# Attention 2's masks: two wide products or eight, replaced by four 64x64 tiles

## The chip, the core and the metric

The kernel runs on one core of a Trainium2 chip. The metric is device time in microseconds (us) of one execution of the whole program, four attention layers and four feed-forward layers, as the median of several runs.

PE is TensorE (PEld its weight loads), DVE VectorE, ACT ScalarE, POOL GpSimd, SP the queue that issues the transfers. SBUF is the working memory, PSUM the one that PE writes (eight banks of 512 f32 columns on 128 partitions).

## The reference

Eight blocks are added to `x` (16 sequences, 128 positions, 128 columns) in turn, each on a layer norm of `x`. The change is in the third attention:

```python
def _L2_xattn_ref(query, key, value, mask, w_q, b_q, w_k, b_k, w_v, b_v, w_o, b_o):
    N_HEAD = 16
    ...
    Q = _split_heads(query @ w_q.T + b_q)
    K = _split_heads(key @ w_k.T + b_k)
    V = _split_heads(value @ w_v.T + b_v)
    scores = jnp.einsum('bhqd,bhkd->bhqk', Q, K) * scale
    scores = jnp.where(mask, -jnp.inf, scores)
    probs = jax.nn.softmax(scores, axis=-1)
    attn = jnp.einsum('bhqk,bhkd->bhqd', probs, V)
    ...
    return merged @ w_o.T + b_o
```

Query and key have 128 positions each, so that the mask of one sequence is 128x128, the same for all 16 heads. A head is 8 wide.

## The kernel before

The program is written by hand as one instruction stream per engine, with semaphores between them. There is no scheduler: the order on an engine is the order of the calls in its block, and an instruction that waits holds back all behind it on that engine. `wait` hangs a wait onto the engine's next instruction; `held` (L266 to L271) gives it a semaphore instruction of its own, which also counts up a semaphore `gate` that nobody reads.

Attention runs as a software pipeline over the 16 sequences, `pipeline(engine, attention_step(layer), ...)` (L222). Step t takes sequence t through its input side (`turn_xn`, `query`), sequence t-2 through the scores (M), t-3 through the turned scores (ST) and the products with the values (AV), and finishes t-4. Two steps of attention 2 are already run inside the feed-forward block before it. Steps 4 to 15 hold all five parts; the last ones have no new sequence.

For a step of attention 2, PE's order is

```python
if Do: AV(2, 1); AV(3, 1)
if Po: shift_turn()
if Mo: M(0)
if Po: ST(0)
if Do: out_turn()
if A: turn_xn()
if Mo: M(1)
if A: query()
if Do and layer == 2: att_turn()
if Po: ST(1)
if Do: out_project()
if Po: AV(0); AV(1)
```

M(0) and M(1) call `scores`, ST(0) and ST(1) `scores_t`; each fills two banks with eight heads, four in each.

- `scores` (L412) writes scores with queries on partitions into banks 0 and 1, of which DVE takes the maxima (L1559, two of 512 columns per call). The mask comes first: `neg_ident`, the identity times -2^100, is the weight and the mask, repeated four times, is streamed: one product of 128x512 for each bank (L417). Then eight products of 48 rows each add the scores (L423), alternately on the upper and the lower half of the array's rows.
- `scores_t` (L428) writes the same scores turned, with keys on partitions, into banks 2 and 3, shifted by the maxima, for ACT's exponential (L874). Here the mask is the weight and `neg_ident` is streamed: eight products of 128x128 (L434). Then products of 48 and 64 rows add the scores (L440) and the shift (L444).

`scores` waits for the maxima of the call before (`mx`); `scores_t` waits for the exponentials that read its banks before (`p`).

In between stand `shift_turn` (L526), `out_turn` (L558, waits for ACT's `att`, L937), `turn_xn` (L507), `query` (L512), `att_turn` (L564, waits for DVE's `att_t`, L1617), `out_project` (L589) and the AV products (L482, 9 columns of weights on each of four strips of the array, whose input `probs` ACT has just written).

DVE's order in a step is: the copy of the turned shift (L1595), the maxima of M(0), statistics of the next sequence (L1526 to L1530), `normalized` (L1613, L1617), the maxima of M(1), the shifts (L1587, L1589), the rest of the query (L1574), the output (L1541). Every fourth step (k % 4 == 0) begins with the statistics of its own sequence, which the output of the step before has to precede; POOL turns them into a deviation (L1197 to L1200), ACT normalizes with it (L931) and then copies `att` (L937).

POOL copies each sequence's mask from bytes (`mask_u8`, loaded once) to bf16 (`mask_bf`, four slots, L1219), then the values (`v_slot`, L1225), computes the next deviation, and splits the query (L1235, L1237). PE's M waits for the copy of its sequence, made two steps earlier (`v`).

The mask is loaded at the start on SP's queue, in the group `later`, as 16x128 pieces of 128 bytes for each of the 128 query positions; DVE waits for the whole group in step 2 of attention 0 (L1434).

Of the kernel before, what the change touches and what calls it, by code (L numbers as in the profile page):

```python
# [14 lines left out]
BF16 = mybir.dt.bfloat16  # L15
U8 = mybir.dt.uint8
# [5 lines left out]
B = 16  # L22
T = 128
D = 128
P = 128
SLOTS = 4
# [8 lines left out]
UNIT = 4  # L35
# [24 lines left out]
def build_kernel(nc, a, out, scratch_q, scratch_k):  # L60
    ctx = ExitStack()
    with ctx:
        def sb(name, shape, dt=F32):
            return ctx.enter_context(nc.sbuf_tensor(name, shape, dt))
# [4 lines left out]
        bank = [ctx.enter_context(nc.psum_tensor(f"bank{i}", [P, 512], F32)) for i in range(8)]  # L69
# [10 lines left out]
        def keep(name, src, shape, dt=F32, group=later):  # L80
            whole = consts[name] = sb("w_" + name, shape, dt)
            group.append((whole[:, :] if len(shape) == 2 else whole[:, :, :], src))
            return whole
# [17 lines left out]
        w2 = keep("w2", a["w2T"], [P, D])  # L101
        b31 = keep("b31", a["L3_ffn_b1"].partition_broadcast(P), [P, F1])
        s_ins = keep("s_ins", a["s_ins"].partition_broadcast(P), [P, 2])
        mask_u8 = keep("mask_u8", a["mask"].rearrange("b q k -> q b k"), [P, B, T], U8)
        BO0, BV1, BV2, BV3, BO2, BF2, B32 = range(7)
        x_sb = sb("x_sb", [P, B, D])
        x_in = a["x"].rearrange("b t d -> t b d")
# [4 lines left out]
        neg_ident = sb("neg_ident", [P, P], BF16)  # L112
# [32 lines left out]
        mx = sb("mx", [P, SLOTS, H1])  # L145
# [4 lines left out]
        rec = sb("rec", [P, SLOTS, H1])  # L150
        att = sb("att", [P, SLOTS, 512])
        att_t = sb("att_t", [P, SLOTS, 512])
        mask_bf = sb("mask_bf", [P, SLOTS, T], BF16)
        v_slot = sb("v_slot", [P, SLOTS, H1, D1 + 1])

        v3_slot = k_parts[:, :, :, :, :].rearrange("p s l j k -> p (s l j k)")[:, 0:SLOTS * 512].bitcast(F32)
# [59 lines left out]
        def wait(eng, s, value):  # L216

            if isinstance(value, int) and value <= 0:
                return
            eng.wait_ge(s, value)  # L220
# [47 lines left out]
        def held(eng, s, value):  # L268

            if isinstance(value, int) and value <= 0:  # L270
                return  # L271
            eng.wait_ge(s, value)
            eng.sem_inc(gate, 1)
# [99 lines left out]
        def _(pe):  # L373
            mm, tr = nc.tensor.matmul, nc.tensor.transpose
# [28 lines left out]
            def turn_probs(sm, n):  # L403

                for u in range(2):
# [3 lines left out]
                        last = tr(bank[2 + u][:, j * T:(j + 1) * T], probs_q[u][:, j * T:(j + 1) * T], ident[:, :])  # L409
                    last.then_inc(sm["st"], 1)  # L410

            def scores(sm, layer, n, s, v):  # L412

                wait(pe, sm["mx"], n)
                if layer == 2:
                    for r in range(2):
                        mm(bank[r][:, :], neg_ident[:, :],  # L417
                           mask_bf[:, s:s + 1, :].to_broadcast([P, UNIT, T]), start=True, stop=False,
                           skip_group_check=True)
                for j in range(UNIT):  # L420
                    for r in range(2):
                        rows, g = slice(64 * r, 64 * r + 6 * D1), v * UNIT + j
                        last = mm(bank[r][:, j * T:(j + 1) * T], q_stack[rows, s, g, :], k_stack[rows, s, g, :],  # L423
                                  start=layer == 1, stop=True, skip_group_check=True)
                        if j == UNIT - 1:
                            last.then_inc(sm["s"], 1)

            def scores_t(sm, layer, n, s, v):  # L428

                wait(pe, sm["p"], n)  # L430
                if layer == 2:
                    for r in range(2):
                        for j in range(UNIT):
                            mm(bank[2 + r][:, j * T:(j + 1) * T], mask_bf[:, s, :], neg_ident[:, :],  # L434
                               start=(j == 0), stop=False, skip_group_check=True)
                for j in range(UNIT):
                    g = v * UNIT + j
                    for r in range(2):
                        rows = slice(64 * r, 64 * r + 6 * D1)
                        mm(bank[2 + r][:, j * T:(j + 1) * T], k_stack[rows, s, g, :], q_stack[rows, s, g, :],  # L440
                           start=layer == 1, stop=False, skip_group_check=True)
                    for r in range(2):
                        rows = slice(64 * r, 64 * r + 64)
                        last = mm(bank[2 + r][:, j * T:(j + 1) * T], pick_bf[rows, g:g + 1].to_broadcast([64, T]),  # L444
                                  shift_t[rows, s, :], start=False, stop=True, skip_group_check=True)
                        if j == UNIT - 1:
                            last.then_inc(sm["st"], 1)
# [711 lines left out]
        def _(pool):  # L1159
# [26 lines left out]
            def attention_step(layer):  # L1186
                sm = S[layer]
                U = (H0 if layer in (0, 3) else H1) // UNIT
                def step(t, k, c):
                    s = k % SLOTS  # L1190
# [25 lines left out]
                    if layer:  # L1216
                        held(pool, sm["av"], (t - 3) * U)
                        if layer == 2:
                            nc.gpsimd.tensor_copy(mask_bf[:, s, :], mask_u8[:, t, :])  # L1219
                        if layer == 3:  # L1220
                            cp = nc.gpsimd.tensor_copy(
                                v3_slot[:, s, :, :, 0:D3].rearrange("p u j e -> p (u j) e"),
# [20 lines left out]
                    elif on(k, 1):  # L1243
                        s = (k - 1) % SLOTS
# [839 lines left out]
```

## Time and profile before

| | us |
|---|---|
| median of 3 runs | 861.32 |
| lowest, highest | 857.58, 863.76 |
| the profiled execution | 858.38 |
| its span, first to last instruction | 856.6 |

| engine | busy us | share of the span |
|---|---|---|
| PE | 581.3 | 68% |
| DVE | 536.8 | 63% |
| ACT | 399.4 | 47% |
| POOL | 255.4 | 30% |

Matmuls are pipelined: a 128-column product is shown with over 0.2 us though the next begins after 0.06, so that spacing, not duration, is what one costs. The clock column is the granted TensorE clock (1.00 is 2.4 GHz, 0.50 is 1.2 GHz). Idle time is put down to what ended last before the instruction began; "issue" is idle time with no such event. All times in rows count from the span's start.

### The profile page before, as it was taken

What the parts mean: (1) busy time and instruction counts of PE and PEld (TensorE: products, weight loads), DVE (VectorE), ACT (ScalarE), POOL (GpSimd) and SP (SyncE); (2) the same over time, 40 slices, a digit from 0 to 9 for tenths busy, and PEclk for the clock granted to TensorE, in tenths of its full rate; (3) what the DMA queues carried; (4) which work ended last, traced back from release to release, by engine and by line L of the source; (5) the groups of instructions that cost most, each with busy time, mean ns of one, the idle gap of its engine ahead of it and who ended that gap; (6) DMA issues with size and microseconds to landing.
All of it is one profiled execution on the core that took longest, in us unless ns stands there. A gap on an engine that the chain in (4) does not pass through costs nothing.

```text
span 856.6 us, 19147 instructions
## 1 busy us (share of the span) xinstructions
PE 581.3 (68%) x5772; PEld 400.5 (47%) x5772; DVE 536.8 (63%) x1653; ACT 399.4 (47%) x893; POOL 255.4 (30%) x515
## 2 busy tenths in 40 slices
PE   4599999987788857878513322699998027875342
PEld 3478787875444444545201101366665015653121
DVE  2477676752677746777688885366675663335673
ACT  1355555561222216666427654555554014445674
POOL 2111111101455533332124226333331113333420
PEclk9989999995999958899655555599999556995555
DMA  8422222220000023334000001133331013550001
GB/s 241 118 63 63 62 61 61 61 56 10 1 0 0 0 56 84 94 101 102 11 0 0 0 0 26 40 87 87 92 88 29 0 29 94 145 142 26 0 2 49
DMA packets 103973, 46.73 MB, mean 55 GB/s; under 512 B 84144, under 2 KB 93424, under 8 KB 103920
## 3 DMA queue, kind: packets, MB, share of 16 engines
q1 hardware_dynamic: 103920, 46.09, 21.5%
q8 instruction: 25, 0.41, 0.2%
q14 instruction: 28, 0.23, 0.1%
HBM read 26.13 MB, written 19.92 MB: 54 GB/s over the span
## 4 chain that ended last, share of the span: by engine, by line
PE 31%; issue 24%; DVE 17%; POOL 9%; DVEq 6%; ACT 5%; DMA 3%; POOLq 3%; SPq 1%; ACTq 0%
PE bank L482 3%; POOL small L1304 2%; PE bank L512 2%; PE bank L423 2%; PE bank L465 2%; PE bank L417 2%; DVE mx L1559 2%; PE bank L434 2%; DVE small L1391 1%; DMA scratch_q<-q_parts 1%; PE bank L586 1%; PE bank L440 1%; PE bank L558 1%; DMA stacks<-scratch_q 1%; POOL stats L1184 1%
## 5 line engine op out<-in xcount | busy, mean ns | idle before, releaser
L1559 DVE TENSOR_REDUCE mx<-bank 128x4 f32<-128x512 f32 x160 | 104.0, 684 | 24.5 <-PE bank L423 22.7
L874 ACT ACTIVATE probs<-bank 128x512 f32<-128x512 f32 x160 | 90.9, 595 | 55.1 <-PE bank L444 50.0
L1184 POOL TENSOR_TENSOR stats<-stats,half_neg 128x1 f32<-128x1 f32 x48 | 26.4, 550 | 186.2 <-DVE stats L1530 178.8
L482 PE MATMUL bank<-probs,v_slot 128*9 128x128 f32 x1024 | 44.5, 288 | 3.4 <-ACT probs L874 0.9
L1574 DVE SCALAR_TENSOR_TENSOR resid<-bank,w_bias_cols,q_parts 128x128 f32<-128x128 f32 x48 | 16.8, 350 | 47.6 <-ACT q_parts L920 47.6
L1541 DVE TENSOR_TENSOR x_sb<-bank,x_sb 128x128 f32 (+1 forms) x64 | 18.5, 289 | 43.5 <-PE bank L586 23.3
L1235 POOL CAST q_parts<-resid 128x128 bf16<-128x128 f32 x48 | 14.2, 296 | 99.2 <-DVE resid L1574 99.2
L906 ACT ACTIVATE xn_t<-bank 128x128 f32<-128x128 f32 x64 | 17.7, 277 | 54.6 <-PE bank L507 52.8
L507 PE MATMUL bank<-w_ident,xn 128*128 128x128 f32 x64 | 21.6, 338 | 31.5 <-DVE xn L1535 20.5
L440 PE MATMUL bank<-stacks 48*128 48x128 bf16 x512 | 39.2, 227 | 2.4 <-DVE shift_t L1595 1.6
L444 PE MATMUL bank<-shift_t,pick_bf 64*128 64x128 bf16 x512 | 39.0, 226 | 0.0
L1063 ACT ACTIVATE att_t<-bank 128x512 f32<-128x512 f32 x16 | 9.6, 597 | 62.3 <-PE bank L747 62.3
L1535 DVE TENSOR_SCALAR xn<-x_sb,stats 128x128 f32 (+1 forms) x48 | 22.0, 458 | 22.7 <-POOL stats L1184 22.7
L937 ACT ACTIVATE att<-bank 128x512 f32<-128x512 f32 (+1 forms) x48 | 25.1, 523 | 23.0 <-PE bank L482 21.2
L423 PE MATMUL bank<-stacks 48*128 48x128 bf16 x512 | 27.9, 234 | 10.0 <-DMA stacks<-scratch_q 7.0
L670 PE MATMUL bank<-ident_bf,yq 128*128 128x128 bf16 x16 | 2.4, 305 | 47.2 <-DVE yq L1724 41.8
L465 PE MATMUL bank<-v,probs 128*128 128x65 f32 x256 | 34.2, 282 | 0.0
L465 PEld LDWEIGHTS bank<-v,probs 128*128 128x128 f32 x256 | 33.4, 205 | 0.0
L1304 POOL TENSOR_TENSOR small<-euler,small 128x8 f32<-128x8 f32 x16 | 26.4, 1648 | 22.8 <-DVE small L1816 22.7
L920 ACT ACTIVATE q_parts<-bank,w_bias_cols 128x128 bf16<-128x128 f32 x48 | 17.6, 367 | 32.6 <-PE bank L512 32.2
L1279 POOL TENSOR_TENSOR probs<-probs,small 128x512 bf16<-128x512 bf16 x16 | 16.5, 1056 | 48.9 <-ACT probs L1023 48.9
L512 PE MATMUL bank<-xn_t,w_proj 128*128 128x128 f32 x96 | 29.0, 392 | 2.6 <-ACT xn_t L906 2.6
(297 smaller groups left out, 1729.1 us busy)
## 6 DMA issues: line engine op xcount, KB each, us to landing
stacks<-scratch_k SPq DMA_DIRECT2D x64, 96.0 KB, 2.2
stacks<-scratch_q SPq DMA_DIRECT2D x64, 96.0 KB, 2.2
scratch_k<-k_parts SPq DMA_DIRECT2D x48, 96.0 KB, 1.8
scratch_q<-q_parts SPq DMA_DIRECT2D x48, 96.0 KB, 1.9
scratch_k<-k_parts SPq DMA_DIRECT2D x48, 64.0 KB, 1.7
scratch_q<-q_parts SPq DMA_DIRECT2D x48, 64.0 KB, 1.8
stacks<-scratch_k SPq DMA_DIRECT2D x16, 192.0 KB, 2.6
stacks<-scratch_q SPq DMA_DIRECT2D x16, 192.0 KB, 2.5
```

The source lines that it names most:

```text
L423: last = mm(bank[r][:, j * T:(j + 1) * T], q_stack[rows, s, g, :], k_stack[rows, s, g, :], start=layer == 1, stop=True, skip_group_check=True)
L440: mm(bank[2 + r][:, j * T:(j + 1) * T], k_stack[rows, s, g, :], q_stack[rows, s, g, :], start=layer == 1, stop=False, skip_group_check=True)
L444: last = mm(bank[2 + r][:, j * T:(j + 1) * T], pick_bf[rows, g:g + 1].to_broadcast([64, T]), shift_t[rows, s, :], start=False, stop=True, ...
L465: last = mm(bank[4 + u % 2][:, j * (D0 + 1):(j + 1) * (D0 + 1)], probs[:, (s * U + u) % 4, j * T:(j + 1) * T], v0[:, s, 2 * j + u, :], sta ...
L482: last = mm(bank[4][32 * j:32 * j + w, cols], v, probs[:, (s * U + u) % 4, j * T:(j + 1) * T], start=layer < 3, stop=True, skip_group_chec ...
L512: mm(q_bank(k)[:, 0:T], wq, xn_t[:, sA, :], start=True, stop=True).then_inc(sm["q_ps"], 1)
L874: activation(probs[:, slot, :], bank[2 + u % 2][:, :], ACT.Tanh if layer == 3 else ACT.Exp, scale=float(d) ** -0.5).then_inc(sm["p"], 1)
L937: activation(att[:, sD, 0:U * T], bank[4][:, 0:U * T], ACT.Copy).then_inc(sm["ot"], 1)
L1184: tt(stats[:, s, 9:10], stats[:, s, 8:9], half_neg[:, :], ALU.pow).then_inc(ln_rstd, 1)
L1304: tt(small[:, s1, 2, 0:E0], euler[:, :], small[:, s1, 1, 0:E0], ALU.pow).then_inc(f["pw"], 1)
L1535: return ts(dst, x_sb[:, t, :], stats[:, s, 6:7], stats[:, s, 9:10], ALU.subtract, ALU.mult)
L1559: reduce(mx[:, sM, at * UNIT:(at + 1) * UNIT], bank[u % 2][:, :].rearrange("p (h k) -> p h k", h=UNIT), AX.X, ALU.max).then_inc(sm["mx"], 1)
```

## The change

Both masks are now made by the same helper, `masks`. It splits the 128x128 product into four of 64x64: rows 0 to 63 and 64 to 127 of the array, each with the upper and the lower half of the output partitions. The weight is always a 64x64 diagonal block of `neg_ident`, and the mask, repeated four times, is streamed, 512 columns. One pair ("straight", rows and outputs of the same half) fills one bank, the other ("crossed") the other bank. A crossed product moves the upper half to the lower, so the mask has to be there with its halves exchanged as well. The turned scores need the mask turned. That makes four forms of it: plain, exchanged, turned, turned and exchanged. They are laid out on the host, loaded as one piece of 8192 bytes per partition, and all four are copied to bf16 by POOL in one instruction of 512 columns. `neg_ident` is no longer streamed anywhere. The waits before these calls become `held`.

```diff
-        mask_u8 = keep("mask_u8", a["mask"].rearrange("b q k -> q b k"), [P, B, T], U8)
+        mask_u8 = keep("mask_u8", a["mask4"], [P, B, 4 * T], U8)
...
-        mask_bf = sb("mask_bf", [P, SLOTS, T], BF16)
+        mask_bf = sb("mask_bf", [P, SLOTS, 4, T], BF16)
...
+            def masks(straight, crossed, i, s):
+                for x, dst in ((0, straight), (1, crossed)):
+                    for half in range(2):
+                        rows = slice(64 * half, 64 * half + 64)
+                        outs = slice(64 * (half ^ x), 64 * (half ^ x) + 64)
+                        mm(dst[outs, :], neg_ident[rows, rows],
+                           mask_bf[rows, s, i + x:i + x + 1, :].to_broadcast([64, UNIT, T]), start=True, stop=False,
+                           skip_group_check=True)
+
             def scores(sm, layer, n, s, v):
-                wait(pe, sm["mx"], n)
                 if layer == 2:
-                    for r in range(2):
-                        mm(bank[r][:, :], neg_ident[:, :],
-                           mask_bf[:, s:s + 1, :].to_broadcast([P, UNIT, T]), start=True, stop=False,
-                           skip_group_check=True)
+                    held(pe, sm["mx"], n)
+                else:
+                    wait(pe, sm["mx"], n)
+                if layer == 2:
+                    masks(bank[0], bank[1], 0, s)
...
             def scores_t(sm, layer, n, s, v):
-                wait(pe, sm["p"], n)
                 if layer == 2:
-                    for r in range(2):
-                        for j in range(UNIT):
-                            mm(bank[2 + r][:, j * T:(j + 1) * T], mask_bf[:, s, :], neg_ident[:, :],
-                               start=(j == 0), stop=False, skip_group_check=True)
+                    held(pe, sm["p"], n)
+                else:
+                    wait(pe, sm["p"], n)
+                if layer == 2:
+                    masks(bank[2], bank[3], 2, s)
...
-                            nc.gpsimd.tensor_copy(mask_bf[:, s, :], mask_u8[:, t, :])
+                            nc.gpsimd.tensor_copy(mask_bf[:, s, :, :].rearrange("p m k -> p (m k)"), mask_u8[:, t, :])
...
-    t["mask"] = g["mask_Bx1xSxS2_bf0"][:, 0]
+    mask = g["mask_Bx1xSxS2_bf0"][:, 0]
+    forms = [m for z in (mask.transpose(1, 0, 2), mask.transpose(2, 0, 1)) for m in (z, np.roll(z, P // 2, 0))]
+    t["mask4"] = np.stack(forms, 2).reshape(P, B, 4 * T)
```

On PE's stream nothing changes its place. At M(0) and ST(0) of a step in the loop's middle there stood before (names are output<-inputs, then columns of weights x streamed columns):

```order
L526 MATMUL bank<-ident_bf,shift 128x128
L220 REGISTER_ALU
L417 MATMUL bank<-mask_bf,neg_ident 128x512 x2
L423 MATMUL bank<-stacks 128x128 x8
L434 MATMUL bank<-neg_ident,mask_bf 128x128 x8
L440 MATMUL bank<-stacks 128x128 x2
```

and now, with the line numbers of the changed kernel (L538 is `shift_turn`, L435 and L452 the scores):

```order
L538 MATMUL bank<-ident_bf,shift 128x128
L273 REGISTER_ALU
L420 MATMUL bank<-mask_bf,neg_ident 64x512 x4
L435 MATMUL bank<-stacks 128x128 x8
L420 MATMUL bank<-mask_bf,neg_ident 64x512 x4
L452 MATMUL bank<-stacks 128x128 x2
```

Two products of 512 columns, and eight of 128, have each become four of 512 on a quarter of the array; the products around them stand as before.

## Rows read from the trace of the kernel before

**Rows 1.** Windows: us; busy us (instructions) of PE, PEld, DVE, ACT, POOL; PEclk; DMA; GB/s
```profile
551.70:560.60 8.90, 8.64 (x104) 5.10 (x104) 4.30 (x12) 3.73 (x7) 2.63 (x8) 0.63 0.27 68
560.60:643.10 82.50, 80.33 (x1337) 54.20 (x1332) 56.94 (x165) 47.15 (x108) 29.68 (x96) 1.00 0.34 87
```
**Rows 2.** Timeline, PE, one ordinary step: start, us, engine, line, operation, tiles, count
```profile
595.50 0.10 PEld L526 LDWEIGHTS bank<-ident_bf,shift 128*128 128x128 bf16 x1 [0.22 <-issue]
595.57 0.59 PE L417 MATMUL bank<-mask_bf,neg_ident 128*128 128x512 bf16 x2
596.10 0.40 PE L423 MATMUL bank<-stacks 48*128 48x128 bf16 x8
596.42 0.62 PE L434 MATMUL bank<-neg_ident,mask_bf 128*128 128x128 bf16 x8
596.98 0.23 PE L440 MATMUL bank<-stacks 48*128 48x128 bf16 x2
...
597.55 0.66 PE L558 MATMUL bank<-w_ident,att 128*128 128x128 f32 x4
...
599.33 0.27 PE L564 MATMUL bank<-w_ident,att_t 128*128 128x128 f32 x1
599.43 0.61 PE L434 MATMUL bank<-neg_ident,mask_bf 128*128 128x128 bf16 x8
599.98 0.23 PE L440 MATMUL bank<-stacks 48*128 48x128 bf16 x2
...
600.96 1.23 PE L482 MATMUL bank<-probs,v_slot 128*9 128x128 f32 x32
602.13 0.23 PE L526 MATMUL bank<-ident_bf,shift 128*128 128x128 bf16 x1
```
**Rows 3.** Instructions that read `mask_bf`: count, duration in ns (min/median/max), first and last start
```profile
L434 PE MATMUL bank<-neg_ident,mask_bf x256: 219/219/314, 553.4 to 659.8; 128*128 128x128 bf16 x128
L417 PE MATMUL bank<-mask_bf,neg_ident x64: 379/379/634, 545.3 to 652.2; 128*128 128x512 bf16 x64
```
**Rows 4.** Timeline, DVE, in the same ordinary step
```profile
596.53 1.29 DVE L1559 TENSOR_REDUCE mx<-bank 128x4 f32<-128x512 f32 x2 [0.53 <-PE bank L423]
...
598.74 0.29 DVE L1617 TENSOR_TENSOR att_t<-bank,rec 128x128 f32<-128x128 f32 x1
599.11 1.29 DVE L1559 TENSOR_REDUCE mx<-bank 128x4 f32<-128x512 f32 x2
```
**Rows 5.** Timeline around a fourth step, all engines
```profile
584.74 1.29 DVE L1559 TENSOR_REDUCE mx<-bank 128x4 f32<-128x512 f32 x2 [0.24 <-PE bank L423]
...
589.77 0.29 POOL L1219 CAST mask_bf<-w_mask_u 128x128 bf16 x1
589.82 0.49 ACT L931 ACTIVATE xn<-x_sb,stats 128x128 f32 x1 [2.45 <-POOL stats L1200]
...
590.93 0.65 PE L558 MATMUL bank<-w_ident,att 128*128 128x128 f32 x4 [0.92 <-ACT att L937]
```
**Rows 6.** Waits, 560.6 to 643.1: who for whom, us in total, times, longest
```profile
POOL stats L1197 <- DVE stats L1530: 15.8, 11, 2.1
```
**Rows 7.** Timeline, PE, the mask and the scores of the second step, at half clock
```profile
551.85 1.04 PE L417 MATMUL bank<-mask_bf,neg_ident 128*128 128x512 bf16 x2
552.82 0.61 PE L423 MATMUL bank<-stacks 48*128 48x128 bf16 x8
```
**Rows 8.** Groups by shape, POOL: busy us, mean ns of one, idle before
```profile
L1246 POOL CAST k_parts<-resid 128x384 bf16<-128x384 f32 x16 | 8.0, 502 | 7.4 <-DVE resid L1677 7.4
```
**Rows 9.** Page, part 2: rate of the transfers in 40 slices of 21.4 us
```profile
GB/s 241 118 63 63 62 61 61 61 56 10 1 0 0 0 56 84 94 101 102 11 0 0 0 0 26 40 87 87 92 88 29 0 29 94 145 142 26 0 2 49
```
**Rows 10.** Timeline, SP and DVE, the last load and the first use of its group
```profile
21.19 0.43 SPq L310 DMA_DIRECT2D stacks<-in_w32T  x1
...
29.57 0.23 DVE L1434 CAST ident_bf<-w_ident 128x128 bf16<-128x128 f32 x1
```
**Rows 11.** Transfers of the first 60 us: issuer, count, size, us to landing
```profile
stacks<-in_w32T SPq DMA_DIRECT2D x1, 256.0 KB, 5.2
```

## The prediction

> **What bounds the kernel now.** I read the windows first, cut at the borders of the stage that the change touches, attention 2. Its 12 undisturbed steps fill one stretch of 82.50 us, 6.9 us each, and PE is busy for 80.33 of it at full clock, while DVE, ACT and POOL are busy 57, 47 and 30 us [rows 1]. A busy PE can still be a waiting PE, so the timeline of PE through one ordinary step comes next [rows 2]. There is hardly a hole in it: each group begins where the streaming of the one before ends, or about 0.10 later. In three of four steps PE sets the pace; in the fourth it waits once for ACT (below). So the price of the masks is to be read on PE, and then what PE meets next.
>
> How the prices come out of [rows 2, 3]. One L417 lasts 0.379 and the pair 0.59, so the second starts 0.21 after the first: that is the streaming of 512 columns at full clock. The pair streams until 595.57+0.43 = 596.00; L423 starts at 596.10. The 0.10 between is a hole that appears where the shape of the tiles on the array changes (128 rows to 48). The eight L434 last 0.62, one 0.219, so they start 0.057 apart and stream 0.45; L440 (again 48 rows) starts 0.56 after the first of them, 0.11 later than needed. Where the shape stays (L564 at 599.33, L434 at 599.43) there is no hole: 0.10 is what L564 streams.
>
> So a mask costs now, up to the first product behind it: M(0) 0.53 (595.57 to 596.10), ST(0) 0.56 (596.42 to 596.98), M(1) the same pair as M(0), 0.53, ST(1) 0.55 (599.43 to 599.98).
>
> **The change, part by part.** *The masks.* Each place gets four products of 64 rows, 64 columns of weights and 512 streamed columns, on four quarters of the array. Does the array run them together? Two halves of the rows do: the eight L423, as wide as L434, last 0.40 where L434, one at a time, last 0.62. Four strips of columns do, with different data streamed through the same rows: 32 L482 take 1.23, although each streams 0.10 or more like L564 (over 3.2 in a row) [rows 2]. Rows and columns split at once do not occur. I take them as together: 0.21 of streaming, 0.02 until the last has started, and loading of the first weights, which nothing covers after a change of shape. For this the four L558 give an upper end: 0.66, of which L564's 0.27 and three starts at 0.11 explain 0.60, so 0.06; 64 columns instead of 128 make about half. Sum 0.26 (0.23 to 0.29), and a hole of 0.10 behind it, 0.36. A second hole is new: M(0), M(1) and ST(1) follow 128-row instructions (L526, L507, L564), whose shape the old mask kept; now 0.10 stands ahead too, 0.46. ST(0) follows L423 and had its hole already. Saved: M(0) 0.07, ST(0) 0.20, M(1) 0.07, ST(1) 0.09; 0.43 per sequence if PE alone counted.
>
> *The held waits.* Each call's wait moves from the mask's weight load to a semaphore instruction of its own on PE. Behind it stand that call's products. Where PE's sequencer is ahead, this costs nothing; it is not ahead at M(0), right behind the wait for `probs`: L526 there idles 0.22 for "issue" [rows 2], 0.12 beyond the hole. One more instruction costs between 0 and that 0.12; I take 0.05, since the new hole runs at the same time. M(0) keeps 0.02.
>
> *What PE meets.* From M(0)'s end to att_turn (L564) DVE works in a row: maxima from 596.53, statistics, then `att_t` until 598.74+0.29 = 599.03, its next maxima at 599.11 [rows 4]. L564 runs at 599.33, 0.30 later; with some 0.05 of hand-over PE can gain 0.25 here, and not the 0.27 of ST(0) and M(1). An ordinary step gains 0.02+0.25+0.09 = 0.36. In the fourth step PE waits 0.92 for `att`, at the end of a chain that comes from the previous step's DVE work through POOL's statistics and ACT's `xn` and `att` [rows 5]. From M(0) of the step before to the end of that wait nothing is gained but what DVE idled before its second maxima, 0.24 [rows 5], however much PE saves. Four steps then gain 0.72 for two whole ordinary ones, 0.02 for M(0) of the third, 0.24 up to the end of the wait, and 0.07+0.09 behind it: 1.14. Three such groups: 3.4.
>
> *Half clock.* The first two steps run partly at 1.2 GHz (mean 0.63 in the second) [rows 1]. There L417 to L423 is 0.97 [rows 7]; new 0.13+0.42+0.05+0.13 = 0.73 (streaming is twice 0.21; the holes are 0.97 less the pair's two 0.42). That is 0.24 for each of four M, by the same count some 0.35 for ST(0), and 0.2 for ST(1), during which the clock rises: 1.5 in all. The full clock comes when it comes; work brought forward in front of it is worth half behind it. I take 1.0 (0.75 to 1.5). The last three steps have no new sequence; DVE is already the later one before L564: 0.1, 0.1 and, with ST(0) behind a wait, 0.3: 0.5.
>
> *POOL's copy*, four times as wide. One of 128 columns takes 0.29 [rows 5], a copy of 384 columns 0.50 [rows 8]; that line goes on to 0.6 for 512, and four times the first would be 1.16: 0.3 to 0.9 more per sequence. Behind it on POOL wait `v_slot` and the next deviation, which waits for DVE for 15.8 us in 11 times anyway [rows 6]; PE needs the copy two steps later. Nothing, while that cover of over 1 us lasts; without it up to 0.9 in each of 16 steps.
>
> *The load*, 1 MB instead of 256 KB. 768 KB at the 241 GB/s of the first slice are 3.2 us [rows 9]. The last load of that group is issued at 21.19 and lands 5.2 later, 26.4; DVE, which waits for all of them, comes to it at 29.57 without idling [rows 10, 11]. Cover 3.2, so nothing; were it gone, 3.2 at most.
>
> Sum: 3.4+1.0+0.5 = 4.9. The profiled execution took 858.38 (span 856.6), so 853.5; the median of the runs, 861.32, lies 2.9 above it, so 856.4. With the low ends (0.23, no cost of the waits, 1.5) a group gains 1.5 and all 6.5; with the high ends (0.29, 0.12) 0.6 and 2.9.
>
> **The rivals.** *The gain goes to DVE and ACT.* If DVE's chain already sets L564 (the 0.30 all hand-over), ordinary steps keep 0.02+0.09, and a group 0.22+0.02+0.16 = 0.4. Three groups, 0.8 of the first steps and 0.4 at the end make 2.4: 858.9. For it: DVE starts its second maxima 0.08 after `att_t`, with no idle time. Against: DVE idles 0.24 there in other steps.
>
> *Two halves of the rows can't write one bank at once (slower).* The new order is straight, straight, crossed, crossed: the two straight products lie on different rows and write one bank, in different partitions. All pairs in the rows (L423, L440) write two banks. If one has to wait for the other, the first straight runs alone, the second beside the first crossed, the last alone: three turns, 0.64+0.03. Then M costs 0.87 instead of 0.53 (0.10+0.67+0.10), ST(0) 0.77 instead of 0.56, ST(1) 0.87 instead of 0.55: 1.2 more per ordinary step, 0.7 in the fourth (0.55 of it falls into the wait), 4.4 a group, 13 for three, 3 at half clock and 2 at the end: 18 slower, 879. It decides from 0.11 more per mask than my 0.26, when the 0.43 per sequence is gone. Against it: straight and crossed leave each partition only one writer per bank. The Trainium skill, TensorEngine Tiling (Array Packing), section Restrictions and Gotchas, speaks for it: different row tiles cannot access the same PSUM bank at once. No run here shows it; by that rule the time would be this rival's.
>
> *More than the sum.* If full clock also comes a step earlier, the second step takes 6.9 like the others instead of 8.90 [rows 1], up to 1.9 more, and with the low ends 8.4: 852.9. Nothing in the rows ties the grant to the masks.
>
> **How the numbers follow.** The sum as it stands: 0.62. Gain lost to DVE: 0.15. Bank shared badly: 0.10. More: 0.07. Small losses, such as holes of 0.2 at the new shape, which would turn the 0.43 per sequence into a loss of 0.4 and the whole into about 4 slower: 0.06. The likeliest gives 856.4. Its own bounds are 854.8 to 858.4; the runs shown lie 3 either side of their median, so a range from 851.8 to 862.0 holds it, the lost gain and most of the rest, and leaves out the bank rival. A measurement of this kernel tells about 1% (8.6 us) from no change. Over 1% faster needs the third rival or a lucky median, 0.11; over 1% slower is the bank rival and a little, 0.11; within 1% 0.78.
>
> **What would show it.** In the changed profile: four mask products starting within 0.03 of each other, and the first product behind them 0.36 later (0.26+0.10); 0.77 would be the bank. Holes of 0.10 ahead of M(0), M(1), ST(1). A short wait of L564 for `att_t`, about 0.02 long, in ordinary steps, which last 6.3 instead of 6.63. The wait before L558 in each fourth step longer than now by some 0.3, since PE gets there 0.56 earlier and the chain 0.24. POOL's copy at 0.6 with nobody waiting for it, and DVE's first cast still at 29.6. The prediction is wrong if the four run in turns, if L564 waits as long as was saved, or if attention 2 shrinks by much more than 5.

## The result, and the profile after

The changed kernel takes 854.64 us (median of 20 runs, 848.81 to 857.90), the kernel before in the same sessions 858.0 (20 runs, 852.31 to 863.76). The ratio is 0.995 with a 95% interval of 0.993 to 0.9969: 2.7 to 6.0 us faster, 4.3 in the middle (the two medians lie 3.4 apart). That is faster beyond the noise, but within the 1% that the prediction set as its bound; the forecast was 856.4, with 4.9 less.

The profiled execution took 851.09 (span 849.3, before 856.6). Line numbers have moved by 12 in most places: L526 is L538, L558 is L570, L564 is L576, L423 is L435, L440 is L452; both masks are L420.

First the timeline of PE through the ordinary step that answers to [rows 2] (start, us, engine, line, operation, tiles, count):

```profile
591.76 0.23 PE L538 MATMUL bank<-ident_bf,shift 128*128 128x128 bf16 x1
591.92 0.41 PE L420 MATMUL bank<-mask_bf,neg_ident 64*64 64x512 bf16 x4
592.27 0.40 PE L435 MATMUL bank<-stacks 48*128 48x128 bf16 x8
592.60 0.41 PE L420 MATMUL bank<-mask_bf,neg_ident 64*64 64x512 bf16 x4
592.94 0.23 PE L452 MATMUL bank<-stacks 48*128 48x128 bf16 x2
...
594.54 0.40 PE L435 MATMUL bank<-stacks 48*128 48x128 bf16 x8
594.87 0.49 PE L524 MATMUL bank<-xn_t,w_proj 128*128 128x128 f32 x2
595.26 0.33 PE L576 MATMUL bank<-w_ident,att_t 128*128 128x128 f32 x1
595.52 0.41 PE L420 MATMUL bank<-mask_bf,neg_ident 64*64 64x512 bf16 x4
595.87 0.23 PE L452 MATMUL bank<-stacks 48*128 48x128 bf16 x2
...
598.01 0.23 PE L538 MATMUL bank<-ident_bf,shift 128*128 128x128 bf16 x1
```

The step lasts 598.01-591.76 = 6.25 instead of 6.63. Four mask products last 0.41 together and one 0.400 (the median of all 256), and in each of the 64 sets they start within 0.01 of each other: the array runs the four quarters at once. The first product behind them starts 0.34 to 0.35 after the first of them, at every place at full clock. From the turn of shifts to the first score M(0) takes 0.51 instead of 0.60, and from M(0)'s scores to ST(0)'s first product 0.67 instead of 0.88 [rows 2].

DVE in the same step and in a later one (same columns; in brackets the idle time before and who ended it):

```profile
592.70 1.29 DVE L1571 TENSOR_REDUCE mx<-bank 128x4 f32<-128x512 f32 x2 [0.44 <-PE bank L435]
593.90 0.28 DVE L1538 BATCH_NORM_STATS2 stats<-x_sb 128x6 f32 x1
...
594.52 0.15 DVE L1542 TENSOR_SCALAR stats<-stats 128x1 f32<-128x1 f32 x1
594.60 0.25 DVE L1625 RECIPROCAL rec<-bank 128x16 f32<-128x16 f32 x1
594.92 0.29 DVE L1629 TENSOR_TENSOR att_t<-bank,rec 128x128 f32<-128x128 f32 x1
595.13 1.28 DVE L1571 TENSOR_REDUCE mx<-bank 128x4 f32<-128x512 f32 x2
...
606.73 0.26 DVE L1625 RECIPROCAL rec<-bank 128x16 f32<-128x16 f32 x1 [0.21 <-PE bank L570]
607.07 0.29 DVE L1629 TENSOR_TENSOR att_t<-bank,rec 128x128 f32<-128x128 f32 x1
607.51 1.29 DVE L1571 TENSOR_REDUCE mx<-bank 128x4 f32<-128x512 f32 x2
```

In the first of these steps DVE puts the statistics of the next sequence (L1538 to L1542) between its maxima and `att_t`, and waits for no other engine from 592.70 on. `att_t` ends at 595.21, and L576 runs at 595.26. Here DVE is now the later one: L576 stands 0.39 behind L524. In the second step there are no statistics in between, DVE waits 0.21 for PE itself, and L576 (607.73) follows L524 (607.40) after 0.33.

The fourth step, on PE:

```profile
585.31 0.41 PE L420 MATMUL bank<-mask_bf,neg_ident 64*64 64x512 bf16 x4 [0.86 <-DMA stacks<-scratch_q]
...
587.39 0.65 PE L570 MATMUL bank<-w_ident,att 128*128 128x128 f32 x4 [0.43 <-ACT att L949]
...
613.57 0.65 PE L570 MATMUL bank<-w_ident,att 128*128 128x128 f32 x4 [1.02 <-ACT att L949]
```

The first of the two waits for its stacks at M(0). In the step before it, the three transfers that write the query out (L360 on SP's queue) take 2.96 us from the first issue to the end of the last, and 1.45 to 2.01 elsewhere in these 13 steps; why, no run shows. What it loses there it doesn't wait later: both fourth steps last the same, 7.54 and 7.53, since ACT's `att` sets their middle either way.

POOL's copy and DVE's first cast, which answer to [rows 5] and [rows 10]:

```profile
578.59 0.61 POOL L1231 CAST mask_bf<-w_mask_u 128x512 bf16 x1
...
29.52 0.23 DVE L1446 CAST ident_bf<-w_ident 128x128 bf16<-128x128 f32 x1
```

Last the windows of attention 2, cut at turns of shifts: the first two steps, in which the clock rises, and the 13 behind them (us; busy us of PE, PEld, DVE, ACT, POOL; granted clock; DMA; GB/s). Of before:

```profile
551.75:567.82 16.07, 15.52 (x215) 9.65 (x216) 9.08 (x26) 7.90 (x17) 5.61 (x18) 0.80 0.30 75
567.82:655.83 88.01, 86.09 (x1442) 57.82 (x1438) 60.83 (x175) 49.01 (x110) 27.24 (x87) 1.00 0.31 80
```

and of after:

```profile
550.53:565.47 14.94, 14.85 (x208) 8.25 (x208) 8.86 (x26) 7.95 (x17) 6.15 (x18) 0.70 0.35 83
565.47:648.55 83.08, 80.42 (x1390) 48.90 (x1386) 59.38 (x175) 49.06 (x110) 31.01 (x87) 1.00 0.34 84
```

The 13 steps at full clock gained 4.9. Of the 7.3 between the two spans 6.06 lie in these 15 steps, 1.2 ahead of the first turn of shifts, and on balance nothing behind the last. The 1.2 aren't foreign to attention 2: the masks of its first sequence stand there. PE starts them at 545.56 (before at 545.29) and comes to the first turn of shifts 4.97 later instead of 6.46, but at a granted clock of 0.84 instead of 0.50 in this stretch, so the products alone don't explain it.

### The profile page after: what moved, and what is told of

The parts are those of the page before. It is cut to its first block, busy times and chain, and to the rows that moved or that the text cites. A ratio compares the mean times of both kernels' runs of the same rounds, so it can differ in the third digit from the quotient of the medians.

```text
span 849.3 us, 19069 instructions
## 1 busy us (share of the span) xinstructions
PE 575.3 (68%) x5708; PEld 390.5 (46%) x5708; DVE 534.3 (63%) x1653; ACT 399.8 (47%) x893; POOL 260.9 (31%) x515
## 4 chain that ended last, share of the span: by engine, by line
PE 30%; issue 23%; DVE 17%; POOL 9%; DVEq 6%; ACT 5%; DMA 5%; POOLq 3%; SPq 2%; ACTq 0%
PE bank L494 3%; PE bank L420 2%; POOL small L1316 2%; DMA scratch_q<-q_parts 2%; PE bank L435 2%; PE bank L524 2%; PE bank L477 2%; DMA stacks<-scratch_q 2%; DVE mx L1571 2%; DVE small L1403 1%; PE bank L598 1%; PE bank L452 1%; PE bank L570 1%; POOL stats L1196 1%; POOLq L1259 1%
## 5 line engine op out<-in xcount | busy, mean ns | idle before, releaser
L1571 DVE TENSOR_REDUCE mx<-bank 128x4 f32<-128x512 f32 x160 | 103.9, 684 | 21.7 <-PE bank L435 20.1
L519 PE MATMUL bank<-w_ident,xn 128*128 128x128 f32 x64 | 21.9, 341 | 31.3 <-DVE xn L1547 20.4
L452 PE MATMUL bank<-stacks 48*128 48x128 bf16 x512 | 40.5, 232 | 2.4 <-DVE shift_t L1607 2.2
L1547 DVE TENSOR_SCALAR xn<-x_sb,stats 128x128 f32 (+1 forms) x48 | 21.3, 443 | 22.5 <-POOL stats L1196 22.5
L435 PE MATMUL bank<-stacks 48*128 48x128 bf16 x512 | 27.8, 234 | 9.8 <-DMA stacks<-scratch_q 7.0
L1316 POOL TENSOR_TENSOR small<-euler,small 128x8 f32<-128x8 f32 x16 | 26.4, 1648 | 22.6 <-DVE small L1828 22.5
L452 PEld LDWEIGHTS bank<-stacks 48*128 48x128 bf16 x512 | 25.7, 101 | 13.7 <-issue 9.8
```

The lines of the kernel that those rows point to most:

```text
L519: tr(dst[:, 0:T], xn[:, sA, :], ident[:, :]).then_inc(ln["xnT_ps"], 1)
L1316: tt(small[:, s1, 2, 0:E0], euler[:, :], small[:, s1, 1, 0:E0], ALU.pow).then_inc(f["pw"], 1)
L1547: return ts(dst, x_sb[:, t, :], stats[:, s, 6:7], stats[:, s, 9:10], ALU.subtract, ALU.mult)
L1571: reduce(mx[:, sM, at * UNIT:(at + 1) * UNIT], bank[u % 2][:, :].rearrange("p (h k) -> p h k", h=UNIT), AX.X, ALU.max).then_inc(sm["mx"], 1)
```

## Experiments

All of them leave everything but attention 2's masks and their neighbours as it is. A step is the distance between two turns of shifts (L526, L538); the three ordinary steps shown are those behind the second fourth step from the start, the same ones in each kernel. The third of them has no statistics between DVE's first maxima and `att_t`; the other two have. The 13 steps are all at full clock (the run without masks: 0.98), and in them one profile tells what the times can't: two profiles of kernels with the same work on PE agree to 0.4 us there, while the whole time of one kernel spreads over 9 to 11.

| kernel | median us | ratio to before (95%) | 13 steps | three ordinary steps | fourth step |
|---|---|---|---|---|---|
| before | 858 to 859 | 1 | 88.0 | 6.63 6.68 6.62 | 7.73 |
| changed | 854.6 | 0.995 (0.993 to 0.9969) | 83.1 | 6.25 6.29 6.12 | 7.53 |
| load and copy only | 858.4 | 0.9991 (0.9968 to 1.0014) | 88.0 | 6.63 6.68 6.62 | 7.73 |
| scores only | 853.9 | 0.9955 (0.9933 to 0.9978) | 86.0 | 6.44 6.50 6.44 | 7.63 |
| turned scores only | 854.6 | 0.9946 (0.9924 to 0.9968) | 84.5 | 6.33 6.39 6.31 | 7.61 |
| no masks | 847.5 | 0.9882 (0.9851 to 0.9912) | 76.7 | 5.56 5.76 5.06 | 7.24 |
| masks twice | 863.5 | 1.0076 (1.0047 to 1.0106) | 92.4 | 6.99 7.03 6.99 | 7.96 |
| bank by rows | 853.3 | 0.9945 (0.9924 to 0.9966) | 83.5 | 6.24 6.33 6.12 | 7.53 |
| scores in quarters | 851.4 | 0.9926 (0.990 to 0.9952) | 82.4 | 6.14 6.23 5.85 | 7.42 |
| all in quarters | 849.0 | 0.9911 (0.988 to 0.9942) | 82.3 | 6.04 6.09 5.75 | 7.37 |
| held waits only | one run | | 88.6 | 6.66 6.79 6.69 | 7.73 |
| half maxima | one run | | 82.4 | 6.12 6.20 6.13 | 7.52 |

**Load and copy alone.** The changed kernel, with PE's masks taken from the first form as before:

```diff
-                    masks(bank[0], bank[1], 0, s)
+                    for r in range(2):
+                        mm(bank[r][:, :], neg_ident[:, :],
+                           mask_bf[:, s, 0:1, :].to_broadcast([P, UNIT, T]), start=True, stop=False, ...)
```

(and the same for the turned scores, from `mask_bf[:, s, 0, :]`; waits as before).

> The four forms of the mask are loaded and copied as in the change, but PE makes its mask products as before, from the first form. Theory (the gain is PE's mask products, load and copy are hidden): no difference to the kernel before, 858 and within 0.3%; ordinary steps of attention 2 stay at 6.62 to 6.68 us, POOL's copy takes 0.61 and nobody waits for it, DVE's first cast stays at 29.5 to 29.6. Rival (part of what was measured comes from, or is lost to, load and copy): a copy that is 0.32 longer and is waited for once a sequence makes 16 x 0.32 = 5 slower, 863; a late load up to 3 slower, seen as idle time ahead of DVE's first cast.

Measured: 0.9991 of before, and every step of the 13 equals that of before to 0.02. The copy takes 0.61, and nobody waits for it. So the two hidden edits cost nothing that can be seen here (by the interval of the times up to 0.3%), and what was gained comes from PE's products.

**The two halves.** Only one of the two calls of `masks` is kept, the other place is as before.

> Only the masks of the scores, M(0) and M(1), by four tiles; those of the turned scores as before. Theory (each place pays for itself): by the prediction an ordinary step is 0.02 + 0.07 = 0.09 shorter than before, 6.55, the whole some 2 us faster, 856; if the held wait and the new hole cost less than I put, up to 0.17 a step and 3 us. Rival (the two halves are not additive, because DVE takes what is saved ahead of L564/L576): this half alone and the other half alone together give clearly more than the 6.1 us that attention 2 gained with both.

> Only the masks of the turned scores, ST(0) and ST(1), by four tiles; those of the scores as before. Theory: an ordinary step is 0.20 + 0.09 = 0.29 shorter, 6.35, the whole some 3.5 to 4 us faster than before, 854.3; the turn of att_t waits for DVE for 0.05 or less. Rival (DVE takes it): the 0.20 of ST(0) turns into a wait of the turn of att_t, the step is only 0.09 shorter and the whole 1.5 faster, 856.5.

Measured in ordinary steps: 0.18 to 0.19 less with the scores, 0.29 to 0.31 less with the turned scores. The first is twice what the prediction put (0.09), the second is what it put (0.29). In the steps with statistics ahead of `att_t` the halves add up to 0.49 and 0.47 (0.19+0.30, 0.18+0.29), and both together gave 0.38 and 0.39; in the step without them they add up to 0.49 and gave 0.50. So 0.1 a step is lost where DVE is the later one, and only there. In the 13 steps the halves gained 2.0 and 3.5, together 5.5, against 4.9. The times (3.9 and 4.6 less than before, by the ratios, and 4.3 with both) are too coarse to tell this.

**Is it DVE?** In attention 2 the maxima are taken over half of each head's scores:

```diff
-                               bank[u % 2][:, :].rearrange("p (h k) -> p h k", h=UNIT), AX.X, ALU.max
+                               bank[u % 2][:, :].rearrange("p (h k) -> p h k", h=UNIT)[:, :, 0:T // 2 if layer == 2 else T],
+                               AX.X, ALU.max
```

> The changed kernel, but in attention 2 DVE takes its maxima over the first 64 of each 128 scores only, so the result of a maximum leaves half of the scores out; each is then some 0.3 shorter. Theory (in the steps of 6.25 to 6.32 DVE is the later one before the turn of att_t, which waits 0.07 for it, and the wait makes PE's sequencer 0.05 late at ST(1)): that wait goes everywhere, and steps of 6.25 become 6.12 to 6.19 like the ones that don't wait now. Rival (PE alone sets the pace, the 0.07 is PE's own): they stay at 6.25. Either way under 2 us on the whole.

Measured: 6.12 6.20 6.13; in the first two the wait is gone. On PE the turn of `att_t` stands 0.33 behind `query` again:

```profile
594.53 0.49 PE L524 MATMUL bank<-xn_t,w_proj 128*128 128x128 f32 x2
594.86 0.27 PE L576 MATMUL bank<-w_ident,att_t 128*128 128x128 f32 x1
```

The step that had no such wait stays at 6.13. The loss is DVE's.

**The held waits by themselves**, in the kernel before:

```diff
-                wait(pe, sm["mx"], n)
+                if layer == 2:
+                    held(pe, sm["mx"], n)
+                else:
+                    wait(pe, sm["mx"], n)
```

(and the same with `p`).

> The kernel before with one thing of the change only: the waits ahead of the masks of scores and turned scores are instructions of their own. Masks, load and copy as before. The prediction put 0.05 for each of these waits where PE's sequencer isn't ahead, at M(0). Theory now (they cost nothing: in the changed kernel the hole ahead of M(0) is 0.107 to 0.15 where it was 0.013 to 0.06, that is one hole of 0.09 at the new shape and no more): ordinary steps 6.62 to 6.68 as before, the hole ahead of the first mask product of M(0) 0.01 to 0.06, ahead of ST(1) 0.01 or less. Rival (the prediction's term): the hole ahead of M(0) is 0.06 to 0.11 and an ordinary step 0.05 longer, 6.70.

Measured: steps 0.03 to 0.11 longer, 0.07 on average; the rival, that is the prediction's term, holds, in this one profile. The cost is at M(0) alone:

```profile
600.73 0.23 PE L532 MATMUL bank<-ident_bf,shift 128*128 128x128 bf16 x1
600.97 0.59 PE L420 MATMUL bank<-mask_bf,neg_ident 128*128 128x512 bf16 x2
```

The mask starts 0.24 behind the turn of shifts in this step and 0.10 and 0.14 in its neighbours, against 0.11 in this step and 0.07 in the others before. In the changed kernel M(0) starts 0.16 or 0.20 behind it in most steps: the hole of the new shape (0.10) and the held wait run at the same time, and what comes on top of the hole is 0.01 to 0.05 there. The reverse, the changed kernel with the waits on the weight loads themselves, wasn't tried.

**What a mask costs now: none, and two.**

```diff
-                if layer == 2:
-                    masks(bank[0], bank[1], 0, s)
```

(both places, and the scores start their banks themselves); and, in the other kernel, each call of `masks` twice.

> The changed kernel without any mask product (load and copy stay; the scores start their banks themselves). Each place then loses 0.34 of mask and, at ST(0), one hole of 0.10 besides: 0.34 + 0.44 + 0.34 + 0.34 = 1.46 a step. Theory (PE sets the pace now, DVE is next and close): what is saved at ST(0) and M(1), 0.78, turns into a wait of the turn of att_t for DVE, and 0.68 remains: ordinary steps 5.6 instead of 6.25, the whole about 10 faster than the changed kernel, 844. Rival (PE alone, DVE still has room): 4.8 a step, 23 faster, 831. Rival (PE is not what bounds): steps stay at 6.2.

> The changed kernel with every set of four mask products issued twice in a row (the second set starts the banks again, so the output stays). Theory (PE sets the pace in ordinary steps and the price of a mask is its streaming): each place grows by the streaming of 512 columns, 0.21, without another hole; four places 0.85 a step, less the 0.12 that PE now loses ahead of the turn of att_t and ahead of ST(1): ordinary steps 6.25 to about 6.98, and the wait of the turn of att_t is gone; the whole about 10 slower than the changed kernel, 865. Rival (DVE sets the pace up to the turn of att_t): only M(0) and ST(1) count, 0.42 a step, 6.67, and 860.

Twice: ordinary steps of 6.99 to 7.03, as PE's own count gave (6.98), 9.3 more in the 13 steps and 8.9 more in the median. With that much more on PE, PE alone sets the pace of ordinary steps, and a set in a place that has its holes already costs its streaming: eight products take 0.56 up to the next, 0.22 more than four.

```profile
595.89 0.63 PE L420 MATMUL bank<-mask_bf,neg_ident 64*64 64x512 bf16 x8
596.45 0.40 PE L436 MATMUL bank<-stacks 48*128 48x128 bf16 x8
```

None: ordinary steps of 5.56 and 5.76 (5.6 expected) and 5.06 where no statistics are in the way; but on the whole some 6 to 7 less than the changed kernel, not 10. Two things were missing in the expectation, and the waits of PE from 560 to 640 us show one of them (who for whom, us in total, times, longest):

```profile
PE bank L433 <- DMA stacks<-scratch_q: 3.1, 3, 1.5
...
PE bank L572 <- DVE att_t L1625: 2.0, 7, 0.3
```

The transfers of the query stacks come late at M(0) in three steps, 3.1 in all. The other is the clock: in this profile the first two steps ran at half clock throughout (granted 0.50, where the changed kernel had 0.70) and took 15.2, although they had less to do, and over its six runs the mean granted clock is 0.781, against 0.789 in the changed kernel's twenty. What that costs in us isn't separated.

**Does it cost anything that two halves of the rows write one bank?** Each half is given one bank, with the same data:

```diff
-                for x, dst in ((0, straight), (1, crossed)):
-                    for half in range(2):
+                for x in range(2):
+                    for half, dst in ((0, straight), (1, crossed)):
```

> The changed kernel, but each half of the rows writes one bank only (rows 0 to 63 write bank 0, rows 64 to 127 bank 1; the data are the same). Theory (two halves of the rows already write one bank at once, in different partitions, at no cost): nothing changes, the first product stands 0.34 behind the first mask product as in the changed kernel, ordinary steps 6.25, the time within 0.3% of 854.6. Rival (sharing a bank costs part of the streaming): the place gets shorter by up to the 0.02 to 0.12 that lie between 0.34 and 0.21 plus a hole, ordinary steps 6.1 or less, 852.

Measured: 0.9945, and the three ordinary steps are the same to 0.04; the first score again stands 0.34 behind the first mask product. Sharing a bank is free here, as long as the partitions differ. Two halves of the rows on the same partitions of one bank weren't tried.

**Is the hole one of shape?** With a bank for each half of the rows, scores too can be cut into 64 columns of weights:

```diff
-                        last = mm(bank[r][:, j * T:(j + 1) * T], q_stack[rows, s, g, :], k_stack[rows, s, g, :],
-                                  start=layer == 1, stop=True, skip_group_check=True)
+                        for o in ((slice(0, 64), slice(64, 128)) if layer == 2 else (slice(0, 128),)):
+                            last = mm(bank[r][o, j * T:(j + 1) * T], q_stack[rows, s, g, o], k_stack[rows, s, g, :],
+                                      start=layer == 1, stop=True, skip_group_check=True)
```

and in a further kernel the turned scores (stacks and `pick_bf`) in the same way.

> As the run with a bank for each half of the rows, and the products of the scores in attention 2 are cut into halves of 64 columns of weights, so that masks and scores have one shape (64 rows, 64 columns) and, by the theory of the hole (it appears where the shape changes), no hole between them, nor between M(0)'s scores and ST(0)'s masks. Theory: M(0) and M(1) 0.10 shorter each, ST(0)'s hole ahead gone as well; DVE starts its maxima 0.10 earlier, so 0.10 of these 0.30 stays and the rest becomes a wait of the turn of att_t, about 0.27 long: ordinary steps 6.15, the whole 1.5 to 2 faster than the changed kernel, 853. Rival (PE can't issue 32 instructions in the 0.23 in which it issues 16 now): each scores group takes up to 0.46, M(0) and M(1) 0.23 longer each less 0.10, ordinary steps up to 6.5, 857.

> As the run before it, and the products of the turned scores (stacks and pick) cut into halves of 64 columns of weights too. Theory of the hole: ST(0) and ST(1) have no hole behind their masks either; of the further 0.20 a step ST(1)'s 0.10 stays, ST(0)'s becomes a wait for DVE: ordinary steps 6.05, the whole 3 faster than the changed kernel, 851.5. Rival (PE can't issue twice the instructions in that time): the 0.47 of turned scores double to 0.94, ordinary steps up to 7.3, 868.

Measured: PE issues twice the products without losing time, and the holes are gone. PE's timeline with all in quarters:

```profile
590.61 0.41 PE L420 MATMUL bank<-mask_bf,neg_ident 64*64 64x512 bf16 x4
590.85 0.40 PE L436 MATMUL bank<-stacks 48*64 48x128 bf16 x16
591.09 0.41 PE L420 MATMUL bank<-mask_bf,neg_ident 64*64 64x512 bf16 x4
591.31 0.25 PE L455 MATMUL bank<-stacks 48*64 48x128 bf16 x4
...
593.28 0.49 PE L529 MATMUL bank<-xn_t,w_proj 128*128 128x128 f32 x2
593.85 0.33 PE L581 MATMUL bank<-w_ident,att_t 128*128 128x128 f32 x1
```

From mask to score it is 0.24 now (0.34 in the changed kernel), from scores to the next mask 0.24 (0.33). Of that, as expected, the two steps with statistics keep 0.06 to 0.11 with the scores alone and 0.20 with both; the rest waits for DVE (L581 stands 0.57 behind L529, not 0.33, and M(1)'s mask 0.33 behind `turn_xn`, not 0.20, 0.15 after the end of the maxima that it waits for). The step without statistics keeps 0.27 and 0.37. The 13 steps fell by only 0.8, though, since PE waited for stacks at three places M(0), 2.9 in all, as in the run without masks. The longest:

```profile
577.26 0.41 PE L420 MATMUL bank<-mask_bf,neg_ident 64*64 64x512 bf16 x4 [1.32 <-DMA stacks<-scratch_q]
```

The changed kernel waits so once, 0.86, and the kernel before never in its 13 steps. Single transfers that write the query out vary in every kernel: the slowest lands 2.73 after its issue before, 3.29 in the changed kernel, 3.76 here. Whether less time to cover them or slower transfers bring the waits, no run separates.

Since the times of the two versions touched, both ran again on one chip.

> The changed kernel itself, timed beside the quartered version on one chip, since the intervals of the two (0.993 to 0.997 and 0.988 to 0.994 of before) touch. Theory (the changed steps stand, only their clock at the start of attention 2 varies): 0.995 of before; the last 13 steps of attention 2, all at full clock, take 83.1 to 83.5 instead of 88.0.

> The version with masks, scores and turned scores all in one shape (64 rows, 64 columns) again. Theory (its holes are gone and 0.10 to 0.2 of a step stay): 0.991 of before and some 0.4% faster than the changed kernel beside it. Rival (what it saves goes to DVE and to the transfers of the stacks, and the first time was lucky): 0.995, like the changed kernel. Where no transfer is late, its ordinary steps are 6.04 to 6.09 again, with the turn of att_t waiting 0.24 for DVE.

Measured: 0.9954 (0.9932 to 0.9977; 83.1 for the 13 steps) for the changed kernel, and 0.9915 (0.9882 to 0.9947; 82.4, again with a late transfer, ordinary steps 6.04 and 6.08) for all in quarters, 851.3 beside 854.8. Both times it stood 0.4% below the changed kernel, some 0.9% below the kernel before. Each pair of intervals still touches, but both hold the noise of the kernel before as well: set against each other, the 12 and the 7 runs on this chip lie 3.2 apart on average (an estimate from their scatter: 1.0 to 5.4), so that the quarters are the faster ones.

## Why the prediction came out

*The mask, 0.26 plus a hole of 0.10.* Right: the next product comes 0.34 to 0.35 later, 0.36 was put. The holes belong to the shape: they are gone where mask and scores have one, and 0.24 is left there.

*Two halves of the rows on one bank.* The rival that would have made it 879 is out: four products start within 0.01 of each other, a second set of four costs 0.22 and not 0.64, and giving each half its own bank changes nothing. The Trainium skill, TensorEngine Tiling (Array Packing), Restrictions and Gotchas, says that different row tiles can't access one bank at once; the rows here show them doing so in different partitions, at no cost. The Trainium skill says on the same page, section Tiling Modes, Key Properties, that a change of the tiling mode drains the engine; the trace agrees, with a hole of 0.10 at each change.

*M(0), 0.02.* Too small: it gained 0.09. The old place had a small hole of its own, which the count left out, and new hole and held wait were added up (0.10+0.05), but run at the same time (0.11 in most steps). The others came near their terms: M(1) gained 0.10 (0.07 put), ST(0) 0.21 (0.20), ST(1) 0.11 (0.09) where PE hasn't waited for `att_t` just before. So alone the scores gave 0.19 (0.02+0.07 put), the turned ones 0.30 (0.20+0.09 put).

*DVE takes what goes beyond 0.25 ahead of L564.* Right where it was read [rows 4]: there PE saves about 0.5 a step and keeps 0.38, for 0.36 put, and with shorter maxima it keeps 0.50. From M(0)'s first score to the turn of `att_t` the step gains 3.23-2.99 = 0.24, for 0.25 put. That the whole step fits to 0.02 is in part luck: M(0) gave 0.07 more than put, and ST(1) behind the wait gave 0.04 instead of 0.09, since its mask stands 0.26 behind L576 there and 0.20 elsewhere.

*The fourth step, and the step before it: the term that failed.* The prediction let nothing be gained from the third step's M(0) to the end of the fourth's wait but 0.24 that DVE idled ahead of its second maxima. The third step's rows, of before, show that DVE idled twice more:

```profile
608.81 0.23 PE L526 MATMUL bank<-ident_bf,shift 128*128 128x128 bf16 x1
609.84 1.29 DVE L1559 TENSOR_REDUCE mx<-bank 128x4 f32<-128x512 f32 x2 [0.54 <-PE bank L423]
611.55 0.26 DVE L1613 RECIPROCAL rec<-bank 128x16 f32<-128x16 f32 x1 [0.42 <-PE bank L558]
...
612.41 1.29 DVE L1559 TENSOR_REDUCE mx<-bank 128x4 f32<-128x512 f32 x2 [0.24 <-PE bank L423]
...
614.57 0.29 DVE L1541 TENSOR_TENSOR x_sb<-bank,x_sb 128x128 f32 x1
```

and of after:

```profile
604.30 0.23 PE L538 MATMUL bank<-ident_bf,shift 128*128 128x128 bf16 x1
...
609.55 0.29 DVE L1553 TENSOR_TENSOR x_sb<-bank,x_sb 128x128 f32 x1
```

In this step no statistics stand between maxima and `att_t`, so that DVE itself waits 0.42 for PE's turn L558. After the change that wait is 0.21, and the second maxima start 3.21 instead of 3.60 into the step. The output of the step, with which the chain to the fourth step's wait begins, starts 5.25 instead of 5.76 into it, 0.51 earlier, as much as PE gained. Third and fourth step together gained 0.50+0.20 where 0.02+0.24+0.16 = 0.42 was put, and a group of four gained 1.47 and 1.43 instead of 1.14. For the same reason the first two of the last three steps, which have no statistics either, gained 0.41 each where 0.1 was put; the third gained 0.23, with 0.3 put. The wait ahead of L570 grew from 0.87 to 1.02 in the undisturbed fourth step at 613.57 (the 0.92 of [rows 5] is that of the other fourth step, which now waits for its stacks), not by 0.3, since the chain gained nearly what PE did.

*Half clock, 1.0.* The prices show, the total doesn't. In the step at the first turn of shifts both kernels stand at half clock (granted 0.50) up to ST(0)'s first product. Of before, with [rows 7] for the first score at 552.82, and of after:

```profile
551.75 0.29 PE L526 MATMUL bank<-ident_bf,shift 128*128 128x128 bf16 x1 [1.17 <-DVE shift L1589]
...
554.33 0.29 PE L440 MATMUL bank<-stacks 48*128 48x128 bf16 x2
```

```profile
550.53 0.29 PE L538 MATMUL bank<-ident_bf,shift 128*128 128x128 bf16 x1 [1.48 <-DVE shift L1601]
...
551.32 0.61 PE L435 MATMUL bank<-stacks 48*128 48x128 bf16 x8
...
552.43 0.29 PE L452 MATMUL bank<-stacks 48*128 48x128 bf16 x2
```

M(0) takes 0.79 instead of 1.07 and ST(0) 1.11 instead of 1.51: 0.28 and 0.40 gained, for 0.24 and 0.35 put. But which work meets which clock differs from run to run. From the first mask product to the 13 steps it took 22.5, 21.7 and 20.4 us in three kernels with the old products on PE or only a held wait more (mean granted clock 0.71, 0.78 and 0.91), and 19.9, 20.3 and 20.7 in the changed one, its repeat and the one with a bank by rows (0.74, 0.73 and 0.68). The means lie 1.2 apart, as 1.0 would have it, but the first three spread over 2.1.

*Copy and load, nothing.* Right: 0.61 for the copy, the first cast at 29.52 instead of 29.57, and 0.9991 for the two alone.

*The sum.* 4.9 was put, 4.3 (2.7 to 6.0) measured. The 13 steps at full clock alone gained 4.9, of which some 3.2 was put (3.4 less the 0.4 of the first fourth step, and 0.2 for two of the last three steps). So full-clock steps gave 1.7 more than put, and the part at half clock doesn't show on top of them in the times: that the total fits is in part luck. One thing that may stand against it is on record, the mean granted clock of whole executions: 0.789 in the changed kernel (20 runs) and 0.790 in its repeat (12), but 0.795 to 0.796 in the kernel before and 0.796 with load and copy, the scores or the turned scores alone. Taking 4.3 us of full clock away accounts for 0.001 of that. Why the rest, and what it costs, no run shows.

The forecast of 856.4 also stood on a median of three runs, 861.32, which twenty runs put at 858.0; 4.9 below that is 853.1. And the range, 851.8 to 862.0, holds 858.0, no change, as well. What bears the prediction out is the price of the mask, the holes and the wait in the rows, more than the time.

## What to carry to other kernels

Price a product in its place, with the hole that each change of tile shape adds (0.10 here, on either side): four quarter tiles took a mask from 0.43 of streaming to 0.22, and wherever the neighbour ahead had the old shape, the new hole ate half of that. Before a wait is taken for the bound of all steps, read the other engine's rows in each kind of step: what stood between maxima and `att_t` in two steps of four decided where 0.1 was lost, and where it wasn't. Where PE gives back time, look at once for the next waits, here DVE and then the transfers of the stacks.

## What was unexpected

Cutting weights of 128 columns into two of 64 doubles the products (16 where 8 were, in the 0.24 from the first of them to the next mask) and costs PE nothing at full clock. A wait in an instruction of its own on PE costs 0.03 to 0.11 a step, in the one profile that has it alone, at the one place where PE's sequencer isn't ahead, and nothing at the three others.
